# First unit's loads dealt out over four steps of the projections, one behind each store

## The reference, cut to what matters

```
x_norm = _layernorm(x, gamma, beta)
q = l2_normalize(heads(x_norm @ w_q)); k = l2_normalize(heads(x_norm @ w_k)); v = heads(x @ w_v)
resonance = 0.5 + 0.5 * tanh((einsum('bhqd,bhkd->bhqk', q, k) - 0.27) * 15)
gate_q, gate_k = (0.25 + 0.75 * sigmoid(einsum('bhtd,d->bht', z, g)) for z, g in ((q, g_q), (k, g_k)))
fused = einsum('bhqk,bhkd->bhqd', resonance * gate_q * gate_k, v)
x = layernorm(x + merge(fused) @ w_o + b_o)
h = silu(fp4(x) @ fp4(w_gate).T) * (fp4(x) @ fp4(w_up).T)
x = layernorm(x + fp4(h) @ fp4(w_down).T)
```

## Time and profile before

| | |
|---|---|
| median of three runs | 4456.29 us (4455.4 to 4465.12) |
| the profiled execution: its own time | 4458.66 us |
| the profiled execution: its span | 4456.9 us |
| PE busy / ACT busy | 4149.7 us (93%) / 4023.4 us (90%) |
| DVE busy / POOL busy | 1561.7 us (35%) / 159.3 us (4%) |
| mean granted clock of TensorE | 0.985 |

### The profile page before, as it was taken

One profiled execution on the slowest core, in us unless ns is written; L12 is line 12 of the kernel. 1 busy time (PEld: TensorE's weight loads), 2 busy tenths in 40 slices (PEclk: granted clock), 3 DMA queues, 4 the chain that ended last, 5 costly groups with the idle time before them and its releaser, 6 DMA issues.

```text
span 4456.9 us, 80908 instructions
## 1 busy us (share of the span) xinstructions
PE 4149.7 (93%) x28776; PEld 1293.5 (29%) x28776; DVE 1561.7 (35%) x4540; ACT 4023.4 (90%) x3271; POOL 159.3 (4%) x120
## 2 busy tenths in 40 slices
PE   7978899999999999999999999999999999999997
PEld 5641222222222222222222222222222222222223
DVE  6754023332333233233332333233323323333236
ACT  4669999999999999999999999999999999999993
POOL 2330000000000000000000000000000000000001
PEclk9999999999999999999999999999999999999998
DMA  3454444334433443344334433443344334433440
GB/s 111 126 124 75 69 75 69 61 62 77 77 57 59 77 77 57 59 77 77 56 61 75 77 56 60 76 77 58 58 76 77 56 61 77 77 54 62 76 81 13
DMA packets 180058, 315.51 MB, mean 71 GB/s; under 512 B 65264, under 2 KB 141808, under 8 KB 154608
## 3 DMA queue, kind: packets, MB, share of 16 engines
q1 hardware_dynamic: 179568, 309.41, 41.2%
HBM read 266.82 MB, written 42.47 MB: 69 GB/s over the span
## 4 chain that ended last, share of the span: by engine, by line
PE 68%; ACT 17%; issue 9%; DVE 4%; SPq 1%; DMA 1%; POOL 0%; ACTq 0%; POOLq 0%; DVEq 0%
PE ps L1267 35%; PE ps L1257 19%; ACT room L696 16%; PE ps L1294 7%; PE ps L1317 4%; DVE room L848 1%; DMA m_f<-fused_t 1%; PE ps L1212 0%; DVE st L802 0%; DVE xnT L838 0%; PE ps L1223 0%; PE ps L1307 0%; SPq L521 0%; PE ps L1204 0%; DVE sm L763 0%
## 5 line engine op out<-in xcount | busy, mean ns | idle before, releaser
L696 ACT ACTIVATE room<-ps 128x1024 f32<-128x1024 f32 (+1 forms) x2816 | 3792.5, 1415 | 235.9 <-PE ps L1257 184.3
L1267 PE MATMUL ps<-room,vt 128*32 128x512 f32 x16384 | 2070.4, 606 | 0.0
L1257 PE MATMUL ps<-qs,room 64*128 64x512 f16 x8198 | 1335.6, 385 | 243.6 <-ACT room L696 221.4
L1257 PEld LDWEIGHTS ps<-qs,room 64*128 64x128 f16 x8198 | 311.1, 94 | 1800.6 <-ACT room L696 1141.6
L1267 PEld LDWEIGHTS ps<-room,vt 128*32 128x32 f32 x16384 | 390.4, 109 | 959.8 <-issue 959.8
L1294 PE MATMUL ps<-wguT,m_xqT 128*128 128x352 f32 x960 | 348.2, 485 | 0.0
L957 DVE TENSOR_TENSOR vz<-ps,vz 128x352 f32<-128x352 f32 x120 | 63.0, 525 | 757.7 <-ACT vz L706 757.7
L962 DVE TENSOR_TENSOR vz<-ps,vz 128x352 f32<-128x352 f32 x120 | 63.0, 525 | 595.8 <-PE ps L1294 595.8
L1317 PE MATMUL ps<-wdnT,wqk 128*128 128x256 f32 x720 | 198.9, 404 | 0.6 <-DVE wqk L927 0.6
L1294 PEld LDWEIGHTS ps<-wguT,m_xqT 128*128 128x128 f32 x960 | 162.6, 189 | 105.2 <-issue 54.3
L590 POOL TENSOR_TENSOR m_x<-m_x,bo 128x256 f32<-128x256 f32 x60 | 43.7, 728 | 3946.9 <-DMA m_x<-in_L_attn_x_dram 3946.9
(11 more groups left out here) (172 smaller groups left out, 2209.1 us busy)
## 6 DMA issues: line engine op xcount, KB each, us to landing
room<-k_parts SPq DMA_DIRECT2D x520, 256.0 KB, 9.3
vt<-v_gated SPq DMA_DIRECT2D x65, 1024.0 KB, 17.5
qs<-q_parts SPq DMA_DIRECT2D x520, 32.0 KB, 10.3
gqb<-q_gates SPq DMA_DIRECT2D x256, 64.0 KB, 2.1
room<-in_L_attn_x_dram SPq DMA_DIRECT2D x16, 512.0 KB, 4.3
v_gated<-vz SPq DMA_DIRECT2D x64, 128.0 KB, 2.1
fused_t<-fs SPq DMA_DIRECT2D x256, 32.0 KB, 1.6
q_parts<-room SPq DMA_DIRECT2D x30, 256.0 KB, 2.8
```

The lines of the kernel that those rows point to most:

```text
L696: act.activation(res[:, c, o:o + m, :], ps[:, o:o + m, :], ACT.Sigmoid, scale=2 * SHARP / QK_UP ** 2, bias=-2 * SHARP * THRESH).then_inc(b ...
L1257: ins = pe.matmul(ps[:, BANK[n % 2] + i, :], ks[o:o + HROWS, par, h // 2, kt * P:(kt + 1) * P], qs[o:o + HROWS, par, h // 2, :], start=Tru ...
L1267: ins = pe.matmul(ps[32 * h:32 * h + 32, SUM_BANK, :], vt[:, par, n * HD:n * HD + 32], r, start=kt == 0, stop=kt == KT - 1, skip_group_che ...
```

## The change

The 17 loads of the first unit leave the head of step 15. `load_unit` now takes a range of loads, and a new function `share(i)` in SP's step issues load number 5 * (k - 12) + i in steps 12 to 15, with i from 0 to 4: behind parts(0), the gates store, parts(1), parts(2) and parts(3). Load numbers 0 to 15 alternate between k and q, number 16 is `vt`, and the last three places stay empty. The wait for the first eight blocks' stores now stands at the head of step 12. So that the steps can differ, steps 12 and 13 are written out on every engine, and the loop covers steps 4 to 11.

```diff
-            with fori(2, NBLK // 2 - 1) as r:
+            with fori(2, NBLK // 2 - 2) as r:
                 for par in range(2):
                     step(2 * r + par, par)
-            for k in range(NBLK - 2, NBLK + 1):
+            for k in range(NBLK - 4, NBLK + 1):
                 step(k, k % 2)
...
             def a_step(k, par):
 
                 m, n = k - 2, k - 1
-                if isinstance(k, int) and k == NBLK - 1:
+                if isinstance(k, int) and k == NBLK - 4:
 
                     for r in range(NR):
                         sp.wait_ge(a_out[r], 16 * QB)
                     sp.wait_ge(a_outv, 16 * NG * QB)
-                    load_unit(0, 0, 0)
+
+                def share(i):
+
+                    if isinstance(k, int) and NBLK - 4 <= k < NBLK:
+                        at = 5 * (k - NBLK + 4) + i
+                        load_unit(0, 0, 0, at, at + 1)
+
...
                     parts(0)
+                    share(0)
                     wait(sp, a_gT, m + 1)
                     sp.dma_start(gqd[m // QB, :, bass.ds((m % QB) * BLK, BLK)], gT[:, :]).then_inc(a_outg, 16)
+                    share(1)
                     parts(1)
+                    share(2)
                     parts(2)
+                    share(3)
...
                 if has(m, 0, NBLK):
                     parts(3)
-
-            def load_unit(j, g, par):
+                    share(4)
+
+            def load_unit(j, g, par, first=0, last=NIN):
...
+                for n in range(first, min(last, NIN)):
+                    if n == NIN - 1:
+                        sp.dma_start(vt[:, par, 0:KT * HG * HD], vd[b, g].rearrange("p k e -> p (k e)"))\
+                          .then_inc(b_in[par], 16)
+                        continue
+                    m, hh = divmod(n // 2, 2)
+                    pk, pq = PAIRS[m]
+                    o = hh * HROWS + m * HD
+                    if n % 2 == 0:
...
+                    else:
...
```

More of the change, by code:

```diff
@@ L467, in load_unit @@
                     sp.wait_ge(a_outg, 16 * NBLK)
[L468 to L471, removed]
+                rows = slice(g * HG * HD, (g + 1) * HG * HD)
+                for n in range(first, min(last, NIN)):
[7 more added lines that the diff above has]
+                    if n % 2 == 0:
                         sp.dma_start(ks[o:o + HD, par],
@@ L477, in load_unit @@
                                      .rearrange("(w e d) t -> e d w t", w=2, e=2)[hh]).then_inc(b_in[par], 16)
-                sp.dma_start(vt[:, par, 0:KT * HG * HD], vd[b, g].rearrange("p k e -> p (k e)"))\
-                  .then_inc(b_in[par], 16)
             a_steps(sp.Fori, a_step)
@@ L871, in _ @@
             at = chain.n
-            with dve.Fori(2, NBLK // 2 - 1) as r:
+            with dve.Fori(2, NBLK // 2 - 2) as r:
                 chain.start(at + (r - 2) * 2 * A_CHAIN)
@@ L877, in _ @@
             chain.start(0)
-            chain.n = at + (NBLK // 2 - 3) * 2 * A_CHAIN
-            for k in range(NBLK - 2, NBLK + 1):
+            chain.n = at + (NBLK // 2 - 4) * 2 * A_CHAIN
+            for k in range(NBLK - 4, NBLK + 1):
                 a_step(k, k % 2)
```

## The result

The changed kernel takes 4436.73 us (median of 6 runs, 4430.29 to 4439.23). The kernel before, run beside it, takes 4461.24 us (6 runs), and 4455.87 us beside the first experiments. The ratio is 0.9946 with a 95% interval of 0.9933 to 0.9959: 0.54% less, 24.5 us by these medians, where 6.8 us had been forecast. The profiled execution's span goes from 4456.9 to 4437.4 us, 19.5 us less.

What follows compares the result with a forecast made beforehand. PE and ACT bound the units; before the first scores, ACT's copies waited for stores behind the load burst. Terms 6.3 + 0.5 = 6.8 us less, the others 0, gave 4449.5 us from the runs' median 4456.29; range 4445 to 4457.5.

Steps and rivals of the forecast that it cites:

- (a): End of projections: without the burst ACT's copies stop waiting for stores, first scores start at 309.03 instead of 315.30, 6.3 us less.
- (b): After the first scores: everything up to the next unit's work moves by the same amount; taken as 0, bound 0 to 0.7 less.
- (c): Projection steps: two more written out instead of looped, 52.10 us becoming 51.62; 0.5 us less, bounds 0 to 0.5.
- (d): Steps 12 to 14: dealt-out loads delay stores behind them on SP's queue, but v_gated has 2.4 us of slack; taken as 0.
- (e): Unit loop standing 38 rows further back on ACT: 13 waits on issue at returns, 34.7 us in total, unchanged; taken as 0.
- The returns change price: Rival at the unit loop's 13 returns: 0.5 us dearer each cancels the gain, 0.2 cheaper is over 0.2% faster; chance 0.09.
- The rule that the prediction takes from the Trainium skill: At unit-loop returns: code streams in blocks of 256 instructions, and a taken branch to a block no longer held fetches it first.
- the sign of being wrong: In the unit loop: ACT's waits on issue, about 35 us in total if right, move by several us.
- late copies: Rival at the projections' end: last k_parts store lands after 308.0, so ACT's copies still end last; 4457.2 us, chance 0.07.
- a starved v_gated: Rival at ACT's L658 heading steps 13 to 15: loads delay v_gated's landing, 4457.3 us or up to 4490; chance 0.06.

Runs made afterwards that it cites:

- the first experiments: Four runs on one chip, with loads in a burst or dealt out and ACT's unit loop at place 7 or 81: 4440.70, 4450.17, 4442.23 and 4450.07 us.
- e10: The changed kernel once more, unaltered, timed on one chip beside two variants and the kernel before: 4434.55 us (0.9947).
- e3: The kernel before with 54 more instructions heading ACT's program, so its unit loop stands at place 7 modulo 128, not 81: 4442.23 us (0.9969).
- e4: The changed kernel with 74 more instructions heading ACT's program, so its unit loop stands at place 81 modulo 128, not 7: 4450.07 us (0.9988).
- e6: The changed kernel with 64 more instructions heading ACT's program, unit loop at place 71 modulo 128; one execution, timed later at 4434.9 us (0.9949).

## Why the prediction was wrong

- **(a), the burst, 6.3 us: right.** 315.30 became 309.04, through the waits named, with DVE's L848 chain as the next in line. The columns of the first table give 4 to 10 us in whole runs.
- **(b), everything behind moves alike: nearly.** TensorE's clock fell as expected; that it would fall a second time, near 327, was not seen, and in this pair of traces 2.5 us of the 6.3 were given back before the first return. As the other traces spread by as much, this is no term of the change.
- **(c), the written-out steps, 0.5 us: right in size.** At the first scores it can't be seen, because this trace of the changed kernel comes to DVE's first instruction of the kind of the earlier trace rows 0.6 us later (22.72 against 22.12). From step to step it can: that instruction steps by 17.29, 17.17 and 17.17 us, 51.63 in all where 51.62 was worked out:

```profile
213.78 1.53 DVE L854 TENSOR_SCALAR xnT<-ps,gam,bet 128x512 f32<-128x512 f32 x2 [3.95 <-PE ps L1239]
231.07 1.53 DVE L854 TENSOR_SCALAR xnT<-ps,gam,bet 128x512 f32<-128x512 f32 x2 [3.85 <-PE ps L1239]
248.24 1.53 DVE L854 TENSOR_SCALAR xnT<-ps,gam,bet 128x512 f32<-128x512 f32 x2 [3.72 <-PE ps L1239]
265.41 1.53 DVE L854 TENSOR_SCALAR xnT<-ps,gam,bet 128x512 f32<-128x512 f32 x2 [3.72 <-PE ps L1239]
```

- **(d), the loads among the stores, 0: right.** In step 14 the four v_gated stores take SP 3.63 us instead of 2.07, and no copy waits for them. Behind the k load that stands directly ahead of v_gated in step 13 the four take SP 2.11 us and land in 2.8 us (median), and ACT's copy waits for DVE as before, not for a store:

```profile
263.73 2.11 SPq L464 DMA_DIRECT2D v_gated<-vz  x4
...
270.55 0.59 ACT L674 COPY room<-ps 128x512 f32<-128x512 f32 x1 [2.34 <-DVE sm L822]
```

- **(e), the moved unit loop, "I take 0": the step that failed.** ACT's gaps at the 13 returns of the earlier trace rows went from 2.67 to 1.70 us each, PE's pause from 2.55 to 1.87, and an iteration from 254.7 to 253.5 us. That is a term of some 13 us less, twice (a). What makes up the 1.2 us of an iteration beyond PE's 0.7 was not separated; between the first and the last return TensorE is also at half the clock for 75 us before, 51 us after and 65 us in e10, where an iteration takes 253.9 us. The text had the mechanism among the rivals ("The returns change price") with the right place and a bound of 34.7 us either way, but gave it a chance of 0.09 and kept it out of the range's lower end. The reason given against it, "body and order in it are unchanged", was no reason: e3 and e4 change neither and move the time by 13 us. The rule that the prediction takes from the Trainium skill was also read too narrowly, as one fetch a return at any place, with a badly placed head only as a thing to come. The head lay badly already: place 81 costs ACT a microsecond more than the others, and e6 shows a place with no fetch. That the waits on issue move by several us is the sign of being wrong that the prediction had named itself; they went from 34.7 us to none.
- The two other rivals, late copies and a starved v_gated, did not happen.

## What to carry to other kernels

When a change adds or removes code ahead of a hardware loop, look for a wait on issue at the loop's returns in the trace, multiply it by the number of returns, and let the range hold that product as a bound: it can go either way with no line of the loop touched. Such a gain says nothing about the change; move the loop alone, with a few dozen idle instructions on one engine, before crediting the edit. And of a burst of loads ahead of stores on one queue, ask which copy waits for those stores: dealt out over earlier steps, the same loads made no copy wait here.

## What was not expected of the hardware

The price of a return on ACT took three values with the place of the loop's code: 2.7 us at place 81, 1.6 to 1.7 us at places 7, 44, 91 and 119, and none at place 71, with 64 instruction packets fewer. Removing ACT's gap altogether gained nothing over the cheap one, because PE's own return (25.3 us in 13 waits) already ended last at the cheap places. Why place 81 is dearer than the other fetching places is not shown; the two packets half a microsecond apart, and the times of the packets at the other places, fit a loop end that asks for the next block just as it goes back.
